# Four buffers in turn for the high and low parts of the projections, and another order of the splat and max products around the last units

## What is computed

```python
q = heads(hidden_states @ Wq); k = heads(hidden_states @ Wk); v = heads(hidden_states @ Wv)
scores = jnp.einsum('bhqd,bhkd->bhqk', q, k) / jnp.sqrt(jnp.float32(D))
attn = jax.nn.softmax(scores, axis=-1)
std = jnp.einsum('bhqk,bhkd->bhqd', attn, v)
...
qa = _affinities(q, positions, directions, scales, ds)   # |q - pos|^2 and (q - pos) . dir
ka = _affinities(k, positions, directions, scales, ds)
w = jnp.einsum('bhqn,hn,bhkn->bhqk', qa, amplitudes, ka)
...
return (1.0 - blend) * std + blend * dgsa
```

## Time and profile before

| | us |
|---|---|
| median of 3 runs | 1472.28 |
| lowest and highest | 1471.37 and 1474.81 |
| the profiled execution | 1475.16 |
| its span, first to last instruction | 1473.4 |

### The profile page before, as it was taken

How to read it: one execution, slowest core, us unless ns; L and a number is a source line. 1 busy time by engine, 2 the same in 40 slices (tenths; PEclk the granted TensorE clock), 3 DMA queues, 4 the chain that set the end, 5 groups by cost and what they waited for, 6 DMA issues and landing times.

```text
span 1473.4 us, 14210 instructions
## 1 busy us (share of the span) xinstructions
PE 1205.4 (82%) x4698; PEld 555.2 (38%) x4698; DVE 1204.3 (82%) x1457; ACT 764.0 (52%) x1118; POOL 164.4 (11%) x211
## 2 busy tenths in 40 slices
PE   5563858688689997898799888889799878877996
PEld 4332323232245443333355433333355423323553
DVE  5878898889979998879889996889799987786223
ACT  6765534436367742546477643555677526352331
POOL 1000111001111120101101110001011111001001
PEclk9775878779879998889799998899799989798998
DMA  6853796556339868444269595462289594540231
GB/s 195 281 173 117 169 250 150 115 129 143 69 99 262 222 166 247 109 115 90 63 156 277 139 243 164 98 160 43 88 226 260 129 243 115 136 113 16 65 101 44
DMA packets 112666, 220.20 MB, mean 149 GB/s; under 512 B 14560, under 2 KB 25312, under 8 KB 112592
## 3 DMA queue, kind: packets, MB, share of 16 engines
q1 hardware_dynamic: 88608, 142.85, 31.8%
q0 software_dynamic: 18432, 67.12, 23.7%
q10 hardware_dynamic: 5552, 9.31, 1.8%
HBM read 122.37 MB, written 29.62 MB: 103 GB/s over the span
## 4 chain that ended last, share of the span: by engine, by line
DVE 41%; PE 25%; issue 10%; DMA 7%; ACT 4%; SPq 2%; POOL 1%; DVEq 0%; ACTq 0%; POOLq 0%
DVE ST L896 15%; DVE ST L888 6%; DVE MX L952 5%; PE ps L1500 5%; PE ps L1307 4%; PE ps L1290 4%; DMA qk_parts<-PT 3%; PE ps L1444 3%; DMA YA<-ST 2%; DVE QAK L1118 2%; PE ps L1460 2%; DVE QS L1105 2%; PE ps L1399 2%; DVE ST L899 2%; DVE BST L932 2%
## 5 line engine op out<-in xcount | busy, mean ns | idle before, releaser
L896 DVE TENSOR_TENSOR_SCAN ST<-dA,ST 128x1024 f32<-128x1024 f32 x128 | 293.0, 2289 | 12.2 <-ACT dA L585 9.6
L1500 PE MATMUL ps<-V,GU 128*128 128x512 f16 x1024 | 240.6, 391 | 5.6 <-DVE V L1092 5.6
L952 DVE TENSOR_REDUCE MX<-ps 128x1 f32<-128x512 f32 x256 | 165.2, 686 | 76.2 <-PE ps L1290 75.9
L501 POOL DMA_DIRECT2D YA<-ST x128 | 109.3, 854 | 969.3 <-DVE ST L899 906.1
L585 ACT ACTIVATE dA<-DL,Aneg 128x511 f32<-128x511 f32 x256 | 168.3, 713 | 65.8 <-DVE ST L896 61.8
L723 ACT ACTIVATE PT<-ps 128x1024 f32<-128x1024 f32 x128 | 126.6, 1021 | 122.0 <-PE ps L1399 121.3
L1290 PE MATMUL ps<-KS,QS 96*128 96x512 f32 x256 | 127.3, 559 | 75.0 <-DVE MX L952 44.2
L899 DVE TENSOR_TENSOR ST<-ST,BC 128x1024 f32<-128x1024 f32 x128 | 156.8, 1225 | 4.4
L888 DVE TENSOR_TENSOR ST<-DU,BC 128x1024 f32<-128x1024 f32 x128 | 155.9, 1218 | 0.3 <-DMA YA<-ST 0.2
L1500 PEld LDWEIGHTS ps<-V,GU 128*128 128x128 bf16 x1024 | 97.6, 100 | 142.5 <-issue 33.8
L1460 PE MATMUL ps<-QS 128*128 128x512 f32 x512 | 140.1, 416 | 2.4 <-DVE QS L1105 1.6
(11 more groups left out here) (229 smaller groups left out, 1536.7 us busy)
## 6 DMA issues: line engine op xcount, KB each, us to landing
YA<-ST POOLq DMA_DIRECT2D x128, 512.0 KB, 7.2
BC<-bc_rows SPq DMA_DIRECT2D x64, 512.0 KB, 8.0
GU<-gu_tiles SPq DMA_DIRECT2D x64, 256.0 KB, 4.7
QS<-proj_tiles SPq DMA_DIRECT2D x64, 256.0 KB, 4.3
qk_parts<-PT ACTq DMA_DIRECT2D x32, 256.0 KB, 4.2
qk_parts<-PT SPq DMA_DIRECT2D x32, 256.0 KB, 5.2
QS<-qk_parts SPq DMA_DIRECT2D x32, 256.0 KB, 4.4
KS<-qk_parts SPq DMA_DIRECT2D x32, 256.0 KB, 5.9
```

What stands on the lines that cost most here:

```text
L896: nc.vector.tensor_tensor_scan(flat, dA[:, a, :, :].rearrange("p e s -> p (e s)"), flat, 0.0, ALU.mult, ALU.add).then_inc(s_scan, 1)
L952: nc.vector.tensor_reduce(MX[:, j % 2, qt, h:h + 1], ps[:, n % 2, :], AX_X, ALU.max).then_inc(s_mx, 1)
L1500: last = mm(ps[:, f % F_RING, :], GU[:, t % GU_RING, k, m * P:(m + 1) * P], XHL[:, z, k, :], start=(k == 0 and z == 0), stop=(k == KT - 1 ...
```

## The change

1. **Buffers.** The high and low parts get four places each by turns: units 0, 1, 4, 5 in PT[:, 1] as before, units 2, 3, 6, 7 in rows 0 to 3 of QAK. s_part becomes four semaphores. The high part and the low part of unit u now wait for the DMAs of unit u - 4. Low part 2 waits for ACT's last reads of the feed-forward phase, splat_affinities and the exponentials of slot 0 for the parts' DMAs.
2. **Order on PE.** All of unit 6 follows unit 5, then splat pair 2, then tiles 0 and 1, then all of unit 7, then tiles 2 to 7. The steps of splat pair 3 stand behind tiles 7, 9 and 11, no longer behind transpose_max. X_FIRST is no longer read on PE; DVE's order stays.

```diff
+        PARTS = (PT[:, 1, :, :].bitcast(F32R), QAK[:, 0:4, :].bitcast(F32R))
+        def high(u):
+            return PARTS[u // 2 % 2][:, u % 2, :]
+        def low(u):
+            return PARTS[u // 2 % 2][:, 2 + u % 2, :]
...
-                    if u >= 2:
-                        act.wait_ge(s_part[u % 2], 32 * KT * b + 32 * (u // 2))
-                    nc.scalar.copy(QKP[:, u % 2, :], bank).then_inc(s_hi, 1)
+                    if u >= 4:
+                        act.wait_ge(s_part[u % 4], 64 * b + 32)
+                    nc.scalar.copy(high(u), bank).then_inc(s_hi, 1)
...
             def splat_affinities(b):
+                dve.wait_ge(s_part[2], 64 * (b + 1))
+                dve.wait_ge(s_part[3], 64 * (b + 1))
...
-                    if u >= 2:
-                        dve.wait_ge(s_part[u % 2], 32 * KT * b + 32 * (u // 2))
+                    if u >= 4:
+                        dve.wait_ge(s_part[u % 4], 64 * b + 32)
+                    if u == 2:
+                        since(dve, s_hh, NT * b)
+                        since(dve, s_sqa, NT * b)
...
                     last.then_inc(s_fill, 1)
-                    max_scores(b, 0, cuts[1], cuts[2])
                     if r >= 2 * KT + 2 and r % 2 == 0:
                         splat_products(b, (r - 2 * KT) // 2 - 1)
-                    max_scores(b, 0, cuts[2], cuts[3])
+                    if r == 4 * KT - 2:
+                        max_scores(b, 0, 0, 2)
+                max_scores(b, 0, 2, 6)
+                for step in range(3):
+                    max_scores(b, 0, 6 + 2 * step, 8 + 2 * step)
+                    splat_products(b, NG - 1, (step,))
+                max_scores(b, 0, 12, 16)
                 transpose_max(b, 0)
-                splat_products(b, NG - 1)
                 max_scores(b, 1, 0, X_AHEAD)
```

More of the change, by code:

```diff
@@ L145, in decoder_layer @@
         s_x, s_fill, s_ev, s_q32, s_hi, s_lo = (sem(n) for n in ("s_x", "s_fill", "s_ev", "s_q32", "s_hi", "s_lo"))
-        s_part = [sem(f"s_part{i}") for i in range(2)]
+        s_part = [sem(f"s_part{i}") for i in range(4)]
         s_gsa, s_dist, s_pj2, s_perp, s_gexp, s_gdir, s_aff = (sem(n) for n in (
@@ L364, in load_stack @@
                 else:
-                    sp.wait_ge(s_part[j], 32 * KT * b + 64)
+                    sp.wait_ge(s_part[j], 64 * b + 32)
+                    sp.wait_ge(s_part[j + 2], 64 * b + 32)
                     if j == 1 and type(b) is int and b == 0:
@@ L390, in attention_phase @@
                     sp.wait_ge(s_lo, 2 * NG * b + u + 1)
-                    sp.dma_start(qk_parts[b, z, P * j:P * j + P, 1 - z, :], QKP[:, 2 + u % 2, :].bitcast(F32)).then_inc(s_part[u % 2], 16)
+                    sp.dma_start(qk_parts[b, z, P * j:P * j + P, 1 - z, :], low(u).bitcast(F32)).then_inc(s_part[u % 4], 16)
                     if u in (2, 3):
@@ L679, in attention_phase @@
                     nc.scalar.square(PT[:, 0, 2 + u % 2, :], bank).then_inc(s_q32, 1)
-                    if u >= 2:
-                        act.wait_ge(s_part[u % 2], 32 * KT * b + 32 * (u // 2))
-                    nc.scalar.copy(QKP[:, u % 2, :], bank).then_inc(s_hi, 1)
+                    if u >= 4:
+                        act.wait_ge(s_part[u % 4], 64 * b + 32)
+                    nc.scalar.copy(high(u), bank).then_inc(s_hi, 1)
                     j, z = UNITS[u]
                     act.wait_ge(s_hi, 2 * NG * b + u + 1)
-                    act.dma_start(qk_parts[b, z, P * j:P * j + P, z, :], QKP[:, u % 2, :].bitcast(F32)).then_inc(s_part[u % 2], 16)
+                    act.dma_start(qk_parts[b, z, P * j:P * j + P, z, :], high(u).bitcast(F32)).then_inc(s_part[u % 4], 16)
                     for place in DECAYS_AT[2 * KT + u]:
@@ L718, in attention_phase @@
                             else:
-                                act.wait_ge(s_part[0], 32 * KT * (b + 1))
-                                act.wait_ge(s_part[1], 32 * KT * (b + 1))
+                                for parts in s_part:
+                                    act.wait_ge(parts, 64 * (b + 1))
                             bank = score_bank(b, j, 2 * p)
@@ L1019, in low_part @@
                     dve.wait_ge(s_hi, 2 * NG * b + u + 1)
-                    if u >= 2:
-                        dve.wait_ge(s_part[u % 2], 32 * KT * b + 32 * (u // 2))
-                    nc.vector.tensor_tensor(QKP[:, 2 + u % 2, :], PT[:, 0, u % 2, :], QKP[:, u % 2, :].bitcast(F32),
+                    if u >= 4:
[3 more added lines that the diff above has]
+                        since(dve, s_sqa, NT * b)
+                    nc.vector.tensor_tensor(low(u), PT[:, 0, u % 2, :], high(u).bitcast(F32),
                                             ALU.subtract).then_inc(s_lo, 1)
@@ L1310, in values, with splat_products @@
                     last.then_inc(s_pv, 1)
-            def splat_products(b, pair):
+            def splat_products(b, pair, steps=(0, 1, 2)):
                 pe.wait_ge(s_q32, 2 * NG * b + 2 * pair + 2)
-                for step in range(3):
+                for step in steps:
                     for u in (2 * pair, 2 * pair + 1):
@@ L1326, in splat_products @@
                             last = mm(ps[rows, 3 + 2 * z, :], dir_bd[:, j, :], q32, start=True, stop=True, **tile)
-                last.then_inc(s_gsa, 1)
+                if steps[-1] == 2:
+                    last.then_inc(s_gsa, 1)
             def bank_free(b, r):
@@ L1360, in attention_phase @@
                         pe.wait_ge(s_ev, 2 * KT * b + KT)
-                    lo, hi = X_FIRST[r - 3 * KT:r - 3 * KT + 2] if r >= 3 * KT else (0, 0)
-                    cuts = [min(lo + n, hi) for n in ((0, 0, 2) if r == 3 * KT + 1 else (0, 2, 4))] + [hi]
                     for k in range(KT):
-                        if k == KT // 2:
-                            max_scores(b, 0, cuts[0], cuts[1])
                         if r < 2 * KT:
```

1 line of the change is left out of this document (removed).

## The result

The changed kernel takes 1460.37 us (median of 6 runs, 1458.29 to 1461.91) against 1472.03 (1470.92 to 1474.81) for the kernel before, run beside it: a ratio of 0.991, with a 95% interval from 0.989 to 0.9927. It is 0.9% faster; 1459.4 was forecast, in a range of 1451 to 1468. The profiled execution took 1458.29 us with a span of 1456.5.

The account below looks back on a forecast made before the run. Bound: PE and DVE waiting for each other, and high parts for stores. Gains 2.5 + 4.7 + 4.3 + 7.5 + 0.8 = 19.8 us, less 4.5 and 2.4 for clock falls, gave 12.9: 1472.28 to 1459.4 us, range 1451 to 1468.

Parts of the forecast that it names:

- the gain up to T: From L (end of low part 4) to T (end of maximum 15): 2.5, 4.7, 4.3 us won in batches 1 to 3.
- the second fall: PE's clock drops between tile 12 and the first score, slowing slot 0: 0.8 us a batch taken, 2.4 in three.
- the first fall: PE's clock drops after thin tiles 2 to 7 behind unit 7: costs 1.5 us a batch, 4.5 in three.
- the walk: Reckoning of PE-DVE hand-overs to the end of maximum 15, at full clock; steps leave 1.05 us delay in batch 1.
- T to S: From end of maximum 15 to first score: sums read 2.5 us earlier, 7.5 us in batches 1 to 3.
- S to Q: First score to end of group 1's 16th maximum, a span marked after measuring; the prediction had no Q.
- Batch 0: First batch, halves between maxima: DVE's 2.43 us wait goes, mostly replaced; 0.8 us won, between 0 and 2.4.
- moves up as a whole: Everything behind the first score in a batch depends only on the kernel's own hand-overs and shifts earlier together.
- the clock holds: Rival: no clock fall in either thin stretch of PE; 19.8 us won, 1452.5 us; chance 0.20.
- The tail eats it: Rival: second fall costs 1.7 and the bias row wait 1.5 us a batch; 1466.6 us; chance 0.15.
- Not the bound: Rival: slot 0 waits for parts or stacks anyway, so only the first score comes earlier; 1472 us; chance 0.07.
- slower: Rival: low clock from unit 6 on makes PE late with unit 7; 1484.9 us; chance 0.08.

Follow-up runs that it names:

- buffers_only: The four buffers of the change with PE's old order, against the kernel before: 1471.0 us, ratio 0.997.
- order_only: PE's new order with the two old buffers, against the kernel before: 1495.17 us, ratio 1.013.
- keep_clock: Changed kernel plus six small unused products on PE around transpose_max, in all batches: 1454.35 us, ratio 0.9855 to the kernel before.
- keep_low5: keep_b123 with low part 5 behind maximum 1 instead of maximum 3 on DVE in batches 1 to 3: 1450.95 us, ratio 0.9815 to the kernel before.
- b0_old_tail: keep_low5_split with batch 0's old order from tile 6 on, splat pair 3 behind the turned maxima: 1447.53 us, ratio 0.9809 to the kernel before.
- sums_first: keep_low5_split with ACT reading the splat sums ahead of the bias row in batches 1 to 3: 1462.05 us, ratio 0.9909 to the kernel before.
- keep_b123: keep_clock with the six small products left out in batch 0: 1452.1 us, ratio 0.9828 to the kernel before.
- keep_low5_split: keep_low5 with tiles 2 and 3 moved into the middle of unit 7 in batches 1 to 3: 1448.01 us, ratio 0.9797 to the kernel before.
- sums_first_y_held: both, with POOL holding its add to YA until the bias row has landed, batches 1 to 3: 1443.42 us, ratio 0.9793 to the kernel before.
- both: keep_low5_split with the edits of sums_first and b0_old_tail together: 1456.71 us, ratio 0.9892 to the kernel before.

## Why the prediction was right

The time came out within 1 us of the forecast, but that it came so near is luck. Two of its terms were mis-sized: the gain up to T by 4.4 us and the loss by the second fall by 5.9 us, both taken too small, and these errors cancel for the most part. Measured again, the same two kernels stood 18.7 us apart instead of 11.7.

- **Buffers.** The waits went, as forecast. `buffers_only` and `order_only` add that the halves of the change alone give ratios of 0.997 and 1.013. What each is worth alone couldn't be read off the trace.
- **Up to T** (11.5 at full clock, less 4.5 for the first fall: 7.0 us). Measured 11.4: 3.8, 3.6 and 4.0 where the walk had 2.5, 4.7 and 4.3 at full clock. As the fall cost batch 2 about 1.5 of this, the gain at full clock is about 12.9 (an estimate), 1.4 more than the walk. The other 3.0 are falls that were reckoned with and didn't come. In the walk a unit was priced at 3.70 us, its record; units 5 and 6 start at 559.74 and splat pair 2 at 566.81, so a unit is 3.5 from start to start. DVE's wait was 2.50 us, not 3.1. In batch 1 T came at L + 14.67 where 16.0 was forecast. The fall of 1.5 us was there only in batch 2 (16.11), with this row for step 0, 1.71 instead of 1.05 us by record:

```profile
888.61 1.71 PE L1335 MATMUL ps<-PT,ones_bd 128*32 128x512 f32 x4
```

  The step that failed is "1.5 us a batch, 4.5 in three". (The six tiles of this stretch are 2.2 us of work by the prediction's own 0.73 for two, not 2.7.) In `keep_clock` all three batches took 16.1 to 16.2, and in batch 1 its clock is at 0.50 here:

```profile
580.00:582.00 2.00, 1.91 (x7) 0.79 0.96 256
582.00:584.00 2.00, 2.00 (x8) 0.50 0.99 275
```

  So the size of 1.5 us was right, but this fall comes in some batches and not in others, and what decides it stays open.
- **T to S** (7.5). Measured 8.0. ACT reads the sums right behind the issue of the bias row (587.28 behind 586.57), the wait of 3.15 us in the earlier trace rows is gone. That the bias row's DMA costs nothing was right for this kernel, with about a us to spare: the first score came 3.23 us behind the issue, which is what ACT's four reads take, and the row had landed 2.33, 1.86 and 2.16 us after it (the last update of its semaphore in the trace). The group 2 row had landed 1.87 us after its issue, so the 4.56 us measured PE's order and not the DMA. Still the row's time is no constant. It took 3.60 us in batch 2 of `keep_low5` and 3.25 in batch 3 of `b0_old_tail`, without an add issued shortly ahead of it, and PE waited for it in both. Why is open. The latter:

```profile
1199.16 0.60 ACTq L644 DMA_DIRECT2D QS<-XD  x1
...
1202.55 0.70 PE L1434 MATMUL ps<-QS,KS 97*128 97x512 f32 x2 [0.20 <-DMA QS<-XD]
```

  The upper bound (4.56 us) was too low for a bad neighbour: 5.1 to 5.4 us from issue to score in `sums_first`, where the row landed 5.0 to 5.2 us after its issue. The figure of the Trainium skill (DMA: Bandwidth & Descriptors, the anatomy of one DMA), about 2.0 us fixed, is fitted to transfers that GpSimd issues. For this row, which ACT issues, the traces agree with it in the changed kernel (1.9 to 2.3 us), and don't in `sums_first`; there the measured time decides.
- **The second fall** (2.4 us in three, bounds 0 to 5.1). Measured 8.3, outside the bounds. This is the term that failed: "a fall there would slow slot 0's first scores and tiles ... 0 to 1.7 us a batch". It came in every batch and lasted 13.6 us. The prediction gives no working for its 1.7 us; the only fall of this kind that it had read, in the earlier trace rows, was over by 592, some 2 us into the dense splat products that the change takes away from there. Its own sign of being wrong, slot 0 longer "by more than a us or two", came true: S to Q grew by 2.7 to 3.0 us. The rule of the Trainium skill that the prediction weighed (TensorE: Matmul & The Clock Gate, on HAM oscillation) was right for this fall, in 3 batches of 3, and held for the first in 1 of 3.
- **Batch 0** (0.8, bounds 0 to 2.4). Measured -0.4 up to Q in one execution and -2.5 in the next; from S to Q it can't be told from its own variation. Up to T the variation is small and something can be said: L to T is 24.6 us before, 23.1 to 23.5 in six profiles with the new order and no products there, and 21.9 in the three kernels with the old order from tile 6 on. So the steps between the tiles cost batch 0 over 1 us of what the rest of the change gives it.
- **What follows S "moves up as a whole".** This is not shown. From L to Q of the four batches the sum is 10.8 us, while the profiled spans differ by 16.9 and the medians by 11.7. From the first projection behind the last slot (L1444 before, L1458 after) to the last feed-forward product (L1500, L1514) of batch 1 the profile of before has 127.26 us, the changed kernel 125.57 and, run again, 124.00. These stretches vary by over a us between executions of one kernel, and what in them is the change's doing stays open.

Of the rivals, "the clock holds" gave 1452.5, and its condition was wrong. `keep_clock` and `keep_b123` took 1454 and 1452, but that doesn't confirm its price: the clock is held there behind T only, the first fall still comes in three and in two batches, and against the kernel before beside them they gain 20.5 and 25.9 us, not 19.8. "The tail eats it" had the fall in every batch right, at too small a price (1.7 for 2.7 to 3.0), and the wait for the bias row wrong (none came); its total was missed because up to T more was won. "Not the bound" and "slower" didn't come; PE stayed dense through unit 7, which was the reason given against the latter, and `order_only` shows what happens once it isn't.

## What to carry to other kernels

A wait of PE that is removed is also a pause that is moved: look at what PE does in the microseconds behind it, for a thin stretch just ahead of dense work costs more than its own idle time, and a few independent products may pay for themselves. Price a loop's work from start to start, not from its record. And a small transfer that someone waits for should be issued ahead of a large one, or the large one held until it has landed.

## What the runs showed of the hardware

- The clock at 0.50 lasted 13.6 us in batch 1 of the changed kernel with PE busy through the last 8 of them (windows above), and ended only at about 598.7; before, a fall in the same place was over by 592. Six products of 256 columns, set between tile 13 and the scores, avoided it in eighteen batches of eighteen (batches 1 to 3 of `keep_clock`, `keep_b123`, `keep_low5`, `keep_low5_split`, `b0_old_tail` and `sums_first_y_held`), at S to Q of 12.79 to 12.83 us. They were not enough once PE stood 1.94 us more (batch 1 of `sums_first`).
- A bias row of 8 KB landed 1.9 to 2.3 us after its issue in batches 1 to 3 of the changed kernel, up to 3.6 us in others (`keep_low5`, batch 2), and 5.0 to 5.3 us when a 512 KB adding transfer had been issued half a us before (`sums_first` and `both`, all six batches).
- Low part 7 on DVE took 1.46 to 1.49 us in batches 1 to 3 of `sums_first`, `both` and `sums_first_y_held` (the row above is one) instead of the 0.68 of low part 4 in the earlier trace rows, while a subtraction of POOL ran beside it. No run takes that apart, so the cause is not shown; it lies on no path that decided here.
